# Attention and a mixture of experts on one core: the pieces of a batch placed anew among its 44 iterations, and their stores after them

## What is computed

```
xn = layernorm(x)
q, k, v = xn @ Wq + bq, xn @ Wk + bk, xn @ Wv + bv            # heads of 16 channels
qc = xn @ Wcq + bcq;  kc, vc = ctx @ Wck + bck, ctx @ Wcv + bcv
y = softmax(causal(q k^T) / 4) v + softmax(qc kc^T / 4) vc
x = x + y @ Wp + bp
z = layernorm(x)
scores = (tanh(z @ gate_w.T) + 1) / 2
for each expert e: its 512 best tokens t:
    add[t] += scores[t, e] * (gelu(layernorm(z[t]) @ fc1[e].T + b1[e]) @ fc2[e].T + b2[e])
x = x + z + add
```

## Time and profile before

| | us |
|---|---|
| median of three runs | 1618.84 (1618.71 to 1629.46) |
| the profiled execution | 1623.42 |
| its span, first to last instruction | 1621.7 |
| busy in the span: PE, DVE, ACT, POOL | 1486.5, 1135.0, 911.5, 550.1 |

### The profile page before, as it was taken

The page is one execution under the profiler, slowest core; times in us unless marked ns, Lnnn a source line. Parts: engine busy times, 40 slices in busy tenths (PEclk is TensorE's granted clock), DMA queues, the critical chain, the costliest instruction groups (busy, mean ns, idle before and its releaser), DMA issues. The chain is left out here.

```text
span 1621.7 us, 26374 instructions
## 1 busy us (share of the span) xinstructions
PE 1486.5 (92%) x8925; PEld 726.8 (45%) x8925; DVE 1135.0 (70%) x3163; ACT 911.5 (56%) x1754; POOL 550.1 (34%) x1005
## 2 busy tenths in 40 slices
PE   8899999999999999999999999999998336999897
PEld 4443443444444444444444344444344223655564
DVE  6868887877887788778778887877850374554441
ACT  2167777677676777776776777777766001121111
POOL 4122333442352334334423533441131202434342
PEclk9599999999999999999999999999999557999999
DMA  6776652855467466728564773666001201443332
GB/s 131 153 137 104 128 81 81 114 117 103 103 115 126 94 93 127 124 79 116 104 116 100 113 130 83 102 122 108 4 3 40 83 1 53 92 114 98 105 87 50
DMA packets 82491, 155.46 MB, mean 96 GB/s; under 512 B 13012, under 2 KB 46420, under 8 KB 82356
## 3 DMA queue, kind: packets, MB, share of 16 engines
q1 hardware_dynamic: 76212, 145.25, 46.4%
q0 software_dynamic: 6144, 8.52, 3.0%
HBM read 96.52 MB, written 53.08 MB: 92 GB/s over the span
## 5 line engine op out<-in xcount | busy, mean ns | idle before, releaser
L827 ACT ACTIVATE probs<-bank_ps 128x512 f32<-128x512 f32 (+1 forms) x1408 | 730.4, 579 | 247.2 <-PE bank_ps L616 238.5
L918 DVE TENSOR_REDUCE chunk_max<-bank_ps 128x1 f32<-128x512 f32 x1024 | 653.5, 683 | 143.4 <-PE bank_ps L655 139.6
L655 PE MATMUL bank_ps<-k_stack,q_stack 62*128 62x512 f32 (+3 forms) x1536 | 536.1, 432 | 7.7 <-DVE chunk_max L918 4.4
L616 PE MATMUL bank_ps<-q_stack,k_stack 64*128 64x512 f32 (+3 forms) x1536 | 511.7, 422 | 26.0 <-ACT probs L827 22.6
L655 PEld LDWEIGHTS bank_ps<-k_stack,q_stack 62*128 62x128 f32 x1536 | 248.2, 191 | 371.3 <-DVE chunk_max L918 201.6
L921 DVE CUSTOM_DVE_ANT_0 masked<-bank_ps,causal 128x128 bf16<-128x128 f32 (+3 forms) x512 | 232.9, 485 | 62.1 <-PE bank_ps L655 58.6
L634 PE MATMUL out_ps<-probs,v_cross 128*32 128x512 f32 x2048 | 274.3, 608 | 0.0
L616 PEld LDWEIGHTS bank_ps<-q_stack,k_stack 64*128 64x128 f32 x1536 | 234.5, 189 | 83.9 <-ACT probs L827 76.5
L1081 POOL TENSOR_TENSOR pool_idle<-pool_idle 128x1 f32<-128x1 f32 x293 | 56.8, 194 | 581.9 <-ACT probs L827 383.5
L1379 ACT ACTIVATE h<-h_ps,b1T 128x512 f32<-128x512 f32 x64 | 44.0, 688 | 270.0 <-PE h_ps L1332 270.0
L1346 PE MATMUL o_ps<-w2T,h 128*128 128x256 f32 x512 | 117.1, 386 | 13.8 <-ACT h L1379 7.0
(11 more groups left out here) (159 smaller groups left out, 1357.1 us busy)
## 6 DMA issues: line engine op xcount, KB each, us to landing
parts_dram<-parts SPq DMA_DIRECT2D x70, 512.0 KB, 2.8
k_stack<-parts_dram SPq DMA_DIRECT2D x180, 192.0 KB, 11.7
q_stack<-parts_dram SPq DMA_DIRECT2D x180, 128.0 KB, 10.6
w1T<-in_L_ffn_fc1s SPq DMA_DIRECT2D x8, 1024.0 KB, 5.7
w2T<-in_L_ffn_fc2s SPq DMA_DIRECT2D x8, 1024.0 KB, 7.6
z_rows<-z_sb SPq DMA_DIRECT2D x8, 528.0 KB, 3.1
x_sb<-in_x SPq DMA_DIRECT2D x8, 512.0 KB, 3.9
ctxT<-in_ctx SPq DMA_DIRECT2D x8, 512.0 KB, 4.8
```

The source lines that it names most:

```text
L616: mm = pe.matmul(bank_of(turn)[:, of.at:of.end], k_stack[base:base + SIDE, g, pair, of.keys:of.keys + P], q_stack[base:base + SIDE, g, pai ...
L655: return pe.matmul(bank[:, 0:n], q_stack[base:base + MAX_ROWS, g, pair, qc:qc + P], k_stack[base:base + MAX_ROWS, g, pair, k0:k0 + n], sta ...
L827: nc.scalar.activation(probs[:, buffer(u, i, p), side, columns], bank_of(("score", g, i, p, side))[:, columns], ACT.Exp, scale=SCALE)\
L918: nc.vector.tensor_reduce(dst, bank[:, 0:n], AX.X, ALU.max).then_inc(max_done, 1)
```

## The change

PLAN is written anew. All 37 pieces stay, and so do the iterations; eight of them now hold two pieces, where two did, and 15 hold none, where nine did. The shift stays at i=7 of every unit; gate moves from (3, 9) to (3, 8). qc, q, kc0, kc1, k is now the order of half 0, and q, kc0, kc1, k, qc that of half 1. HALF_ORDER reads these orders from PLAN, and number_of, project and the wait in store_parts go by it; EARLY (here 1) is the number of half 1's pieces ahead of (2, 7). SP sends the shift of the next unit 0 ahead of fill(2), no longer behind it. PE's wait for y0T1 stands before q, qc and k of half 0.

```
 PLAN = {
-    (0, 1): (("out_cross", 0),), (0, 2): (("v", 1),), (0, 3): (("out_self", 0),), (0, 4): (("vc0", 1),),
-    (0, 5): (("vc1", 1),), (0, 6): (("yT0", 0),), (0, 7): (("shift", 0),), (0, 8): (("yT1", 0),),
-    (0, 9): (("y0T0", 0), ("y0T1", 0)), (0, 10): (("q", 0),),
-    (1, 0): (("qc", 0),), (1, 1): (("k", 0),), (1, 3): (("kc0", 0),), (1, 4): (("out_cross", 0),),
-    (1, 5): (("out_self", 0),), (1, 6): (("kc1", 0),), (1, 7): (("shift", 0),), (1, 10): (("proj0", 0),),
-    (2, 0): (("proj1", 0),), (2, 2): (("q", 1),), (2, 4): (("out_cross", 0),), (2, 5): (("out_self", 0),),
-    (2, 6): (("vc0", 0),), (2, 7): (("shift", 0),), (2, 8): (("qc", 1),), (2, 10): (("k", 1),),
-    (3, 0): (("kc0", 1),), (3, 1): (("kc1", 1),), (3, 2): (("v", 0),), (3, 4): (("out_cross", 0),),
-    (3, 5): (("out_self", 0),), (3, 6): (("vc1", 0),), (3, 7): (("shift", 0), ("zT0", 0)),
-    (3, 8): (("zT1", 0),), (3, 9): (("gate", 0),),
+    (0, 2): (("vc0", 1),), (0, 3): (("out_cross", 0), ("out_self", 0)), (0, 4): (("v", 1),),
+    (0, 5): (("y0T0", 0), ("y0T1", 0)), (0, 6): (("vc1", 1),), (0, 7): (("shift", 0), ("qc", 0)),
+    (0, 8): (("yT0", 0),), (0, 9): (("q", 0),), (0, 10): (("kc0", 0),), (1, 0): (("kc1", 0),), (1, 1): (("yT1", 0),),
+    (1, 2): (("out_cross", 0),), (1, 3): (("k", 0),), (1, 5): (("out_self", 0),),
+    (1, 7): (("shift", 0), ("proj0", 0)), (2, 1): (("proj1", 0),), (2, 2): (("q", 1),), (2, 3): (("out_cross", 0),),
+    (2, 7): (("shift", 0), ("v", 0)), (2, 8): (("out_self", 0),), (2, 9): (("kc0", 1),), (2, 10): (("zT0", 0),),
+    (3, 0): (("kc1", 1),), (3, 2): (("out_cross", 0),), (3, 3): (("k", 1), ("vc0", 0)), (3, 5): (("qc", 1),),
+    (3, 6): (("out_self", 0), ("zT1", 0)), (3, 7): (("shift", 0),), (3, 8): (("gate", 0), ("vc1", 0)),
 }
+EARLY = sum(half == 1 and name in HALF_PIECES and place < (2, 7) for place, names in PLAN.items() for name, half in names)
+HALF_ORDER = tuple(tuple(name for _, names in sorted(PLAN.items()) for name, half in names
+                         if name in HALF_PIECES and half == hf) for hf in range(2))
...
-            return 2 * len(HALF_PIECES) * piece.of + len(HALF_PIECES) * piece.half + HALF_PIECES.index(piece.name)
+            order = HALF_PIECES if piece.of == 0 else HALF_ORDER[piece.half]
+            return 2 * len(HALF_PIECES) * piece.of + len(HALF_PIECES) * piece.half + order.index(piece.name)
...
-                if stacked and name == HALF_PIECES[0]:
+                if stacked and name == HALF_ORDER[hf][0]:
...
-                    project(("q", "qc", "k", "kc0", "kc1"), 0)
+                    project(HALF_ORDER[0], 0)
...
-                    project(("q",), 1)
+                    project(HALF_ORDER[1][:EARLY], 1)
                 put_shift(3, 4 * b + 3)
                 if not last:
-                    project(("qc", "k", "kc0", "kc1"), 1)
+                    project(HALF_ORDER[1][EARLY:], 1)
+                    put_shift(0, 4 * b + 4)
                     fill(2, 2 * b + 4, N_EXP * (4 * b + 3))
-                    put_shift(0, 4 * b + 4)
...
-                            if at[2:] == ("q", 0):
+                            if at[2:] in (("q", 0), ("qc", 0), ("k", 0)):
                                 pe.wait_ge(*freed(find_piece(b, first, last, "y0T1")))
```

## The result

| | before | changed |
|---|---|---|
| median of 20 timed runs each, us | 1622.7 | 1617.66 |
| ratio, 95% interval | | 0.9963 [0.9948, 0.9978] |
| profiled span, us | 1621.7 | 1611.8 |
| the eight batches, first score product of the first to the last slot of the last, two profiles each, us | 1177.8, 1174.5 | 1166.6, 1166.2 |

The account below looks back on a forecast made before the run. PE was taken as the bound, losing time only in gaps between its instructions. Gap terms summed to +0.9 us a batch, +5 for six full batches, -1 for the end batches: +4, giving 1623 us, range 1608 to 1639.

Parts of the forecast that it names:

- PE's gaps: Per slot, its length above PE's work without its piece: 0.36 us at i=1, 0.50 at i=3, 0.44 at i=10.
- the floors of the piece-free slots: Slots without a piece wait on the score banks behind ACT's exps: 2.49 (i=1), 2.70 (i=3), 2.93 us (i=10).
- My sum: Gaps added up over a full batch: +0.9 us, bounds -0.3 and +2.3; six full batches +5 us.
- The statistics, +0.6: Statistics in piece-free slots (1,10), (2,0), (3,1), (3,4): DVE work of about 2.8 us costs +0.6 a batch, between 0 and 1.0.
- The second piece at the price of a lone one: In slots with two pieces, each was charged its work from rows where it stood alone, such as 0.59 us for four transposes.
- the gap of transposes alone at i=6: From (0,6) with yT0 alone: 3.20-0.59-2.33 = 0.28 us; transposes alone stay at three slots, counted as 0.
- the piece-free slots against the gaps that go: Piece-free slots from 9 to 15, +1.88 us a batch; against it shifts alone -1.08, (3,7) -0.92, (3,5) -0.49.
- Batches 0 and 7: First and last batch lack pieces, gain some and lose some: -1 us together, within 3 either way.
- The DMA chain: SP's queue from the shift store to unit 1's shift rows, landing at +36.5 to +38.5 us: just holds, 0.7 to 3 us to spare.
- the rival with the late chain: Chain needs 5 us more, PE stalls at kc0 or (1,0) in six batches: 18 us, 1641; chance 0.14.
- slack: Rival: piece-free slots run at PE's own work after long slots, -4.8 us a batch, six times -29, 1590; chance 0.08.
- the clock: Rival: half-clock episodes at all seven batch ends, +5 us, 1628, chance 0.08; none at all, -6, 1617.

## Why the prediction was wrong in sign

**What held.** Where the time is lost (PE's gaps, by slot), the floors of the piece-free slots, 3.25 for a shift alone, 4.18 for qc with the statistics in (3,5) (forecast 4.2), 5.31 for gate with vc1 (5.32). fill(2) behind the shift is needed. No wait for the context, none of the kind that the semaphore counts could bring.

**What failed.** My sum was +0.9 us a full batch, within -0.3 and +2.3; the measured one is -1.1. (The bounds don't follow from the terms either, whose own bounds add up to +0.1 and +3.0.) The 2.0 us between are three terms:

- *The statistics, +0.6.* Measured nothing: (1,10) 2.74, (2,0) 2.49, (3,1) 2.49, and (3,4) 2.70. I had compared DVE's work of 2.8 us with the slot's length, and took the ring of four banks for a loan that is soon used up. It lasts longer than that: in the run with twice the reductions DVE passed the added work on to the slots behind at no cost in these, and it counted only in (2,3) and (3,2), which hold a piece.
- *The second piece at the price of a lone one.* I took PE's work for a piece from rows in which it stood alone, and added two of them. With the prediction's costs and measured, in us: (0,3) 3.38, 3.22; (0,5) 3.81 (3.7 in its list of unit 0's slots), 3.65; (0,7) 4.97, 4.85; (1,7) 4.62, 4.53; (2,7) 5.05, 4.93; (3,3) 5.20, 5.01; (3,6) 3.51, 3.36; (3,8) 5.32, 5.31. Together 1.0 us less. The timeline of the changed kernel in (0,3) shows it for the transposes:

```profile
814.14 0.86 PEld L672 LDWEIGHTS bank_ps<-ident,u_sb 128*128 128x128 f32 x8 [0.36 <-issue]
815.16 0.18 PEld L661 LDWEIGHTS bank_ps<-k_stack,q_stack 62*128 62x128 f32 x1 [0.17 <-issue]
```

Eight in a row take from 814.14 to 815.16, 1.02 us; four alone took 0.59, so the second four cost 0.43. I read from this that the change from one kind of product to another, with the 0.17 of "issue" at its end, is paid once a slot and not once a piece. The addition of yT0 beside vc1 (0.53 for 0.59) says the same, smaller. No run measured the change of kinds apart from the pieces.
- *The slots at i=10.* (1,10) 2.74 for the 2.93 of (3,10), (2,10) 3.13 for 3.36: 0.4 together. For (1,10) I had taken the floor from the one free slot of that i that before had. PE is busy for 2.68 in it and for 2.53 in (1,10). What makes unit 3 longer there I didn't find out. For (2,10), zT0 alone, I had taken the gap of transposes alone at i=6, 0.28; here it is 0.05, and no run says why.

Without the statistics the prediction's own terms come to +0.3 (the piece-free slots against the gaps that go); less 1.0 and 0.4 they give the -1.1.

**Batches 0 and 7.** I took -1 together, within 3. Over two profiles each they went from 283.7 to 282.0 us, -1.7; part of that is the one wait of 1.6 us in before's batch 0. This held.

**The DMA chain.** Here the working was nearly right, and its upper end came true. The shift's store went out at -11.45 (forecast -11.5), fill(2) at -8.6 (-8.8), the two stores were over at 13.0 (12.5 to 13.5), the rows landed at 38.75 (36.5 to 38.5). PE, though, is faster than I had it: it would have been at (1,0) at 35.1 + 3.53 = 38.7 and not 39.2. So of the 0.7 to 3 us nothing was left. That is the first step of the rival with the late chain, at a price of 2.1 to 2.4 us a run instead of 18.

**The whole.** Over the eight batches, the mean of two profiles each, 1176.15 us became 1166.4: -9.75. Of these -6.3 are the clean batches (five times -1.14, and -0.6 in batch 6, which has no token statistics in (3,5) and took 147.4 before), -1.7 the two ends, -5.4 what before had above its clean batches (5.1 of it seven falls of the clock in two profiles), and +3.6 what the changed kernel has above its own (2.1 to 2.4 of it waiting for the shift, 1.3 one fall of the clock in each, in the first profile behind such a wait); rounding leaves 0.1. Timed, it is -6.0 [-8.4, -3.6], and -8.3 [-12.5, -4.2] the second time. Without the clock's share, -5.1 + 1.3 = -3.8, the -9.75 would be about -6. The first timing holds -6 and leaves out -9.7, the second holds both. Of the rivals, slack is refuted by the 2.70 that stayed, and the clock stays open.

## What to carry over

Where a loop has a floor in each turn, count the floors and what fills them before you count the work; but price the second piece in a turn from a row in which two stand together, since part of what a lone piece costs is the change of kinds. Before an engine is blamed for a stretch in which it is busy throughout, double its work there. And when a small transfer is moved ahead in a queue in fixed order, follow the queue to the next one that PE waits for: a plan that is faster on PE uses up its spare from the other side, and here sending a fill behind the next such transfer gave back 2 to 4 us.

## What the hardware showed that I had not expected

- **The clock falls more often beside one order than another, and no single neighbour explains it.** In three profiles with the old places the granted clock fell in (3,9), at the gate's 16 narrow matmuls, in 11 of 18 full batches. In six with the new places and gate beside vc1 in (3,8), the run with the 10 us waits left aside, it fell there in 4 of 36. gate alone in (3,9) of the new order had 1 of 6, gate with vc1 in the old 2 of 6, gate behind the shift in (3,7) 3 of 6. What PE did before each of these falls was a slot with the gate, PE busy throughout or nearly, and the level in (3,10) behind a fall in (3,9) was often 0.50, which is 1.2 GHz, and else 0.66 to 0.84 on average or, once, full. The gate isn't needed for a fall: in two runs with the old places it came in (3,7) of batch 0, which has no gate, in two with the new in (0,7) of batch 7, and in the changed kernel's first profile in (1,0) of batch 3, behind 1.05 us of waiting for the shift's rows. How much of the timed gain comes from this stays open: between nothing and 3.8 us (5.1 less the 1.3 that the changed kernel still loses to falls), and no run held the clock up without also moving a piece.
- **A free slot behind a wait of 10 us runs at half clock.** With fill(2) ahead of the shift, (0,0) took 3.69 or 3.70 us, for 2.43, at a granted clock of 0.50 behind the wait in (3,10), in all seven batches that had one.
- **A 32 KB store on SP's queue takes as long as what is ahead of it.** The same store landed in 1.5 us with the queue empty (793.84 to 795.31), and in 10.3 us behind fill(3) and the context (830.77 to 841.05), just behind fill(3)'s last part (839.89) and the context (840.88). The ring order of the Trainium skill (DMA: Bandwidth & Descriptors, Queues, rings and completion order) agrees with both, and with the 1.5 us of the same store (827.54 to 829.01) in the run that sent fill(3) behind it.
